# Padding the SBUF layout of a two-layer attention and feed-forward kernel to multiples of 64 bytes

## The chip, the cores and the metric

The program runs on one core of a Trainium2 chip. The metric is device time in microseconds (us), here the median of three runs. The profile is of one execution of the same program.

## The reference, cut to what matters

```python
x = x + _L0_xattn_ref(_layernorm(x), ctx_4096, Wq, bq, Wk, bk, Wv, bv, Wo, bo)  # 16-wide window, 8 heads
x = x + _L0_ffn_ref(_layernorm(x), Wg, Wu, Wd, ag, au, ad)                      # silu(gate) * up, inner width 1376
x = x + _L1_xattn_ref(_layernorm(x), ctx_4096, ctx_4096, pos, mask, Wq, Wk, Wv, Wo)  # 32 heads, 8 key/value heads, rotary
x = x + _L1_ffn_ref(_layernorm(x), gate_w, expert_w)                            # top 2 of 8 experts
```

`x` is 16 x 64 tokens of 512 float32 values, that is 8 tiles of 128 tokens. All four steps keep float32 accuracy.

## The kernel before, in words

The kernel is four stages in a row, each with its own order of work for every engine: `window_attention`, `gated_ffn`, `cross_attention` and `routed_ffn`. All large products are made by the helper `mm3` (lines 121 to 123): each operand is kept as a high and a low part of type float32r, and three matmuls (high by high, high by low, low by high) give the accurate product. A matmul names its stationary operand first (the weights that are loaded into the array) and its moving operand second (the one that streams through). The profile writes them the other way round: `PS<-NTh,W` has NTh moving and W stationary. Each matmul of the kernel has its own weight load.

The forms that the prediction speaks of, all with 128 x 128 stationary operands:

- **Keys and values** of the cross attention: `wkv` moves (256 columns), the context `CTh`/`CTl` is stationary.
- **Queries** of the cross attention: the normed rows `NTh`/`NTl` move (256 columns), the weights in `W` are stationary.
- **Output** of the cross attention: `W` moves (512 columns), `ca_aTh`/`ca_aTl` is stationary.
- **Gate and up** of the gated feed-forward: `NTh`/`NTl` move (512 columns), `W` is stationary. **Down**: `W` moves (512 columns), a part of `W` or `ff_hl` is stationary.
- **Experts** of the routed feed-forward: `W` moves (512 columns), `NTh`/`NTl` is stationary.

The cross attention is a loop over 64 units (8 key/value groups by 8 tiles), software-pipelined so that in one turn TensorE makes the keys, values and queries of unit n, the scores of n-2, the attention product of n-3 and the output of n-4. The gated stage loops over 11 chunks of the inner width, the routed one over 23 tiles of tokens. Between them the other engines split operands into parts (ACT high, DVE or POOL low), apply the rotary table and the softmax, and load weights (SP's queue).

SBUF buffers are placed one behind the other in the order in which the program asks for them (`two_layers_kernel`, from line 1994), each at the next multiple of 32 bytes within a partition; what a stage asks for is given back at its end. `X` begins at byte 16512, a multiple of 64. `const` has 164 floats (656 bytes) and begins at a multiple of 64 too, so what comes behind it begins 32 past one: `NTh` at 33568, then `NTl`, `CTh`, `CTl`. The six small buffers of `NormedRows.buffers` take 224 bytes, three and a half times 64, so `qT` (99328) and `room` (107520) are at multiples of 64 again. `room` has `GatedInputs.SIZE` = 3606 floats and turns the offset once more: `CTX` or `W` (121952), `ca_raw`, `ca_kvraw`, `ca_cosT`, `ca_sinT`, `ca_cap`, the `rf_gw` and `ca_wkv` parts, `ff_hl` and most buffers of the window attention begin 32 past a multiple of 64. In the cross attention `mx`, `su` and `rc` (96 bytes) bring `ca_aTh` and `ca_aTl` to a multiple of 64 (224832).

So before the change every float32r operand that moves through TensorE begins 32 bytes past a multiple of 64, and all of them step by multiples of 512 bytes within their buffer. Of the float32r stationary operands all do but `ca_aTh` and `ca_aTl`.

Of the kernel before, what the change touches and what calls it, by code (L numbers as in the profile page):

```python
# [20 lines left out]
F32 = mybir.dt.float32  # L21
F32R = mybir.dt.float32r
# [6 lines left out]
P = 128  # L29
BATCH, SEQ, E = 16, 64, 512  # L30
# [3 lines left out]


WARM_UP = 7
WH, WD, WIN = 8, 8, 16
BLK = 16
KEYS = 2 * BLK
# [5 lines left out]
IT = -(-INTER // P)  # L45

HEADS, KVH, HD = 32, 8, 128
GRP = HEADS // KVH
# [87 lines left out]
def views(room, *sizes):  # L136

    ends = np.cumsum(sizes).tolist()
    return [room[:, end - size:end] for end, size in zip(ends, sizes)]


def allocator(nc, stack):
    def sb(name, shape, dt=F32):
        return stack.enter_context(nc.sbuf_tensor(name, shape, dt))

    def sem(name):
        return stack.enter_context(nc.semaphore(name))

    return sb, sem
# [131 lines left out]
def window_attention(nc, sh, d, norm, ffn):  # L281
# [13 lines left out]
    with ExitStack() as st:  # L295
        sb, sem = allocator(nc, st)
# [44 lines left out]
        S = {x: sem("wa_" + x) for x in names}  # L341

        with nc.Block() as block:
            @block.sync
            def _(sp):
                def load(dst, name, done, a, b):
                    sp.dma_start(dst[:, a:b, :], d[name][2 * a:2 * b, :, :].rearrange("(t b) s e -> (b s) t e", b=2)
                                 ).then_inc(done[a], 16)

                load(sh.X, "x", x_loaded, *LOADS[0])  # L350
                sp.dma_start(sh.const[:], d["consts"][:, :C_BASE]).then_inc(S["const_loaded"], 16)
                for i, w in enumerate(("Wq", "Wk", "Wv", "Wo")):
                    sp.dma_start(wrow[:, i, :], d["L0_" + w]).then_inc(S["loaded"], 16)
                    sp.dma_start(brow[i:i + 1, :], d["L0_b" + w[1]].rearrange("(a c) -> a c", a=1)).then_inc(S["loaded"], 16)
                load(sh.CTX, "ctx", ctx_loaded, *LOADS[0])
                for b2 in range(2):
                    sp.dma_start(bv_row[:, b2 * SEQ:(b2 + 1) * SEQ], d["L0_bv"].rearrange("(a c) -> a c", a=1)
                                 ).then_inc(S["bv_loaded"], 16)
                load(sh.X, "x", x_loaded, *LOADS[1])
                load(sh.CTX, "ctx", ctx_loaded, *LOADS[1])  # L360
                sp.wait_ge(S["zeroed"], 2)
                sp.wait_ge(S["const_loaded"], 16)
                sp.dma_start(d["blank"][0:P, :], blank[:]).then_inc(S["const_loaded"], 16)
                sp.wait_ge(S["const_loaded"], 32)
                for k in range(1, 4):
                    sp.dma_start(d["blank"][k * P:(k + 1) * P, :], blank[:]).then_inc(S["const_loaded"], 16)
                ffn.first_loads(sp)
                sp.wait_ge(S["const_loaded"], 80)

            @block.tensor  # L370
            def _(pe):


                pe.wait_ge(S["zeroed"], 1)
                for _ in range(WARM_UP):
                    nc.tensor.matmul(PJ, wT[:, 0, :], wT[:].rearrange("p a b -> p (a b)"), start=True, stop=True)
# [375 lines left out]
class GatedInputs:  # L752

    SIZE = 7 * E + 2 * IT

    def __init__(self, nc, st, room, d):
        sem = allocator(nc, st)[1]
# [418 lines left out]
def cross_attention(nc, sh, d, norm, next_norm, cross):  # L1178
# [11 lines left out]
    with ExitStack() as st:  # L1190
        sb, sem = allocator(nc, st)
# [10 lines left out]
        kT = kT.rearrange("p (a k) -> p a k", a=2)  # L1202

        qT = sh.qT[:].rearrange("p (a h b x) -> p a h b x", a=2, h=2, b=4)
        mx, su, rc = (sb("ca_" + x, [P, 2, 4]) for x in ("mx", "su", "rc"))
        aT = [sb(f"ca_aT{part}", [P, GRP, P], F32R) for part in ("h", "l")]

        QT = sh.PS[:, 0, :]
        KT = sh.PS[:, 1, 0:PAIR]
# [8 lines left out]
        S = {x: sem("ca_" + x) for x in names}  # L1218
# [775 lines left out]
def two_layers_kernel(nc, d):  # L1994
    with ExitStack() as st:
        sh = Shared()
        sh.X = st.enter_context(nc.sbuf_tensor("X", [P, TT, E], F32))
        sh.const = st.enter_context(nc.sbuf_tensor("const", [P, C_BASE], F32))
        sh.PS = st.enter_context(nc.psum_tensor("PS", [P, 8, 512], F32))
        sh.NTh, sh.NTl, sh.CTh, sh.CTl = (  # L2000
            st.enter_context(nc.sbuf_tensor(x, [P, EC, TT * P], F32R)) for x in ("NTh", "NTl", "CTh", "CTl"))
        d["blank"] = nc.dram_tensor("blank", (4 * P, E), F32).ap()
        d["slots"], d["outs"] = (nc.dram_tensor(x, (rows, E), F32).ap()
                                 for x, rows in (("slots", EXPERTS * CAP), ("outs", SLOT_TILES * P)))
        sh.norm_buffers = NormedRows.buffers(allocator(nc, st)[0])
        sh.qT = st.enter_context(nc.sbuf_tensor("qT", [P, 4 * E], F32))
        norm1, norm2 = (NormedRows(nc, sh, st, name, views(sh.qT, E, E, E, E)[2:]) for name in ("n1", "n2"))
        sh.room = st.enter_context(nc.sbuf_tensor("room", [P, GatedInputs.SIZE], F32))
        ffn = GatedInputs(nc, st, sh.room, d)
        with nc.sbuf_tensor("CTX", [P, TT, E], F32) as sh.CTX:  # L2010
            spent = window_attention(nc, sh, d, norm1, ffn)
        sh.W = st.enter_context(nc.sbuf_tensor("W", [P, RING, 2, EC, E], F32R))
        cross = CrossInputs(nc, sh, st, d)
        q_rows = views(sh.qT, E, E, E, E)
        norm3 = NormedRows(nc, sh, st, "n3", q_rows[:2] + views(cross.cosT, E, E) + views(cross.sinT, E, E) + q_rows[2:])
        gated_ffn(nc, sh, d, norm1, ffn, norm2, cross, spent)
        cross_attention(nc, sh, d, norm2, norm3, cross)
        routed_ffn(nc, sh, d, norm3, cross)
# [28 lines left out]
```

## Time and profile before

| | |
|---|---|
| median of 3 runs | 1142.0 us (1138.05, 1142.0 and 1142.47) |
| span of the profiled execution, first to last instruction | 1134.8 us |
| what the three timed runs have beyond that span | 3.3 to 7.7 us |
| busy PE, PEld (weight loads), DVE, ACT, POOL | 1043.0, 866.0, 662.1, 385.0, 499.3 us |
| mean granted TensorE clock | 0.965 of full speed |

The page names the profiled execution by its span and does not say which of the timed runs stands beside it, so its own time is that span plus an unknown few microseconds. Busy shares are read against the span. A matmul's own duration in the profile has a modelled end and overlaps the next one; how fast matmuls follow each other is read from their starts in the timeline.

### The profile page before, as it was taken

The numbers are of one execution on the slowest core, as the hardware profiler recorded it, in microseconds if no ns is written. First come the engines' busy times: TensorE is split into PE (matmuls) and PEld (weight loads), VectorE is DVE, ScalarE is ACT, GpSimd is POOL, SyncE is SP. The second block draws the span as 40 slices with busy tenths as digits, with TensorE's granted clock in tenths as the row PEclk, the third lists the DMA queues.
The fourth block names the chain that finished last, engine by engine and source line by source line (L and its number), as shares of the span: only waits on it lengthen the run. The fifth ranks groups of instructions, "written<-read, shape, count | busy, mean of one in ns | idle before, by whom it ended". The sixth has DMA issues, their size and how long they took to land. (4 is left out here: it accounts for less than half of the span.)

```text
span 1134.8 us, 24062 instructions
## 1 busy us (share of the span) xinstructions
PE 1043.0 (92%) x9170; PEld 866.0 (76%) x9170; DVE 662.1 (58%) x1383; ACT 385.0 (34%) x875; POOL 499.3 (44%) x567
## 2 busy tenths in 40 slices
PE   7889888999999889999999999999999999755994
PEld 3666677788887678888888888888888888533783
DVE  5787874544454676556565655656565565850324
ACT  4687864222222332222222222222222221520331
POOL 3444441342223345545444554444454542137745
PEclk9899998999999889999999999999999999986997
DMA  6100004573642021111111011111011100036768
GB/s 227 33 3 4 3 4 122 186 262 134 234 149 85 10 84 29 51 34 45 31 29 48 29 28 57 28 49 28 29 47 28 38 11 1 1 115 208 248 219 275
DMA packets 51807, 92.07 MB, mean 81 GB/s; under 512 B 10749, under 2 KB 24317, under 8 KB 51261
## 3 DMA queue, kind: packets, MB, share of 16 engines
q1 hardware_dynamic: 42108, 69.13, 19.5%
q10 hardware_dynamic: 6624, 12.06, 3.2%
q0 software_dynamic: 2976, 9.44, 2.5%
q8 instruction: 76, 1.25, 0.5%
q14 instruction: 23, 0.18, 0.1%
HBM read 77.25 MB, written 36.18 MB: 100 GB/s over the span
## 5 line engine op out<-in xcount | busy, mean ns | idle before, releaser
L121 PE MATMUL PS<-NTh,W 128*128 128x256 f32 (+2 forms) x688 | 216.7, 315 | 0.0
L123 PE MATMUL PS<-NTh,W 128*128 128x256 f32 (+2 forms) x688 | 214.1, 311 | 0.0
L122 PE MATMUL PS<-NTl,W 128*128 128x256 f32 (+2 forms) x688 | 214.1, 311 | 0.0
L122 PEld LDWEIGHTS PS<-NTl,W 128*128 128x128 f32 (+1 forms) x688 | 131.1, 191 | 7.0
L123 PEld LDWEIGHTS PS<-NTh,W 128*128 128x128 f32 (+1 forms) x688 | 129.3, 188 | 8.5
L121 PEld LDWEIGHTS PS<-NTh,W 128*128 128x128 f32 (+1 forms) x688 | 129.6, 188 | 7.2
L1509 POOL TENSOR_TENSOR W<-ca_raw,W 128x512 fp32r<-128x512 f32 x64 | 82.5, 1290 | 114.5 <-ACT W L1359 114.5
L1447 DVE TENSOR_REDUCE ca_su<-room 128x4 f32<-128x256 f32 x64 | 26.9, 420 | 155.4 <-ACT room L1375 155.4
L1476 DVE TENSOR_TENSOR room<-PS,ca_sinT 64x512 f32<-64x512 f32 (+1 forms) x192 | 115.1, 600 | 2.6
L121 PE MATMUL PS<-W,ca_aTh 128*128 128x512 f32 x256 | 106.3, 415 | 3.5 <-DVE X L1464 3.5
L1375 ACT ACTIVATE room<-room 128x256 f32<-128x256 f32 x64 | 26.8, 419 | 222.6 <-POOL room L1556 222.6
L122 PE MATMUL PS<-W,ca_aTh 128*128 128x512 f32 x256 | 100.9, 394 | 0.0
L123 PE MATMUL PS<-W,ca_aTl 128*128 128x512 f32 x256 | 100.6, 393 | 0.0
L1546 POOL TENSOR_TENSOR qT<-room 128x512 f32<-128x512 f32 x64 | 81.8, 1278 | 26.6 <-DVE room L1476 26.3
L1476 DVE TENSOR_TENSOR room<-PS,ca_cosT 128x512 f32<-128x512 f32 (+1 forms) x96 | 57.8, 603 | 56.4 <-PE PS L1298 55.9
L1006 DVE TENSOR_TENSOR X<-X,PS 128x512 f32<-128x512 f32 x88 | 60.3, 687 | 48.9 <-PE PS L123 48.4
L1049 POOL TENSOR_TENSOR ff_hl<-ff_hf,W 128x512 fp32r<-128x512 f32 (+1 forms) x22 | 28.6, 1302 | 134.0 <-ACT W L943 134.0
L1399 ACT ACTIVATE room<-PS 128x256 f32<-128x256 f32 x64 | 24.6, 385 | 182.1 <-PE PS L1324 182.1
L121 PE MATMUL PS<-ca_wkvh,CTh 128*128 128x256 f32 x256 | 78.9, 308 | 1.9 <-issue 1.7
L1533 POOL TENSOR_TENSOR room<-room,ca_rc 128x256 f32<-128x256 f32 x64 | 39.2, 613 | 82.2 <-DVE ca_rc L1449 82.2
L123 PE MATMUL PS<-ca_wkvh,CTl 128*128 128x256 f32 x256 | 72.1, 282 | 0.0
L122 PE MATMUL PS<-ca_wkvl,CTh 128*128 128x256 f32 x256 | 71.9, 281 | 0.0
(258 smaller groups left out, 2366.8 us busy)
## 6 DMA issues: line engine op xcount, KB each, us to landing
ca_raw<-in_L_Wq SPq DMA_DIRECT2D x32, 256.0 KB, 2.8
ca_raw<-in_L_Wo SPq DMA_DIRECT2D x32, 256.0 KB, 2.6
rf_raw<-in_experts SPq DMA_DIRECT2D x28, 256.0 KB, 3.6
room<-slots ACTq DMA_DIRECT2D x23, 256.0 KB, 3.2
outs<-room ACTq DMA_DIRECT2D x23, 256.0 KB, 3.3
outs<-blank SPq DMA_DIRECT2D x11, 512.0 KB, 8.9
room<-in_L_Wg SPq DMA_DIRECT2D x10, 256.0 KB, 2.7
room<-in_L_Wu SPq DMA_DIRECT2D x10, 256.0 KB, 3.0
```

The costliest lines, as they stand in the source:

```text
L121: nc.tensor.matmul(out, l_hi, r_hi, start=first, stop=False)
L122: nc.tensor.matmul(out, l_hi, r_lo, start=False, stop=False)
L123: return nc.tensor.matmul(out, l_lo, r_hi, start=False, stop=last)
L1006: nc.vector.tensor_tensor(sh.X[:, t, :], sh.X[:, t, :], D[:, t % 4, :], ALU.add).then_inc(S["added"], 1)
L1049: nc.gpsimd.tensor_tensor(hl[:w, slot, tok], hf[:w, half, :], hh[:w, slot, tok].bitcast(F32), ALU.subtract).then_inc(S["h_split"], 1)
L1375: nc.scalar.activation(s, s, ACT.Exp).then_inc(S["exped"], 1)
L1399: nc.scalar.activation(pT, PP, ACT.Copy).then_inc(S["pp_copied"], 1)
L1447: nc.vector.reduce_sum(su[:, w, :], sm[:, w, :, :], AX_X).then_inc(S["summed"], 1)
L1476: return nc.vector.tensor_tensor(out[out_rows, some].rearrange("p (m k) -> p m k", m=count), x[rows, :].rearrange("p (m k) -> p m k", m=co ...
L1509: return nc.gpsimd.tensor_tensor(dst[1], src, dst[0].bitcast(F32), ALU.subtract)
L1533: nc.gpsimd.tensor_tensor(s, s, rc[:, w, :].unsqueeze(2).broadcast_to([P, 4, SEQ]), ALU.mult).then_inc(S["probs"], 1)
L1546: last = nc.gpsimd.tensor_tensor(qT[:, slot, j, :, :].rearrange("p b (m q) -> p m b q", m=2), *parts, ALU.add)
```

## The change

Four buffers change size or place. `const` grows from 164 to 176 floats, with the load writing the first 164 as before; 8 floats that nobody uses follow the small buffers of the norm; `room` grows from 3606 to 3616 floats; and `ca_aTh`, `ca_aTl` are asked for ahead of `mx`, `su` and `rc` instead of behind them. No instruction is added, removed or moved in any queue.

```diff
+LINE = 16
...
-                sp.dma_start(sh.const[:], d["consts"][:, :C_BASE]).then_inc(S["const_loaded"], 16)
+                sp.dma_start(sh.const[:, 0:C_BASE], d["consts"][:, :C_BASE]).then_inc(S["const_loaded"], 16)
...
-    SIZE = 7 * E + 2 * IT
+    SIZE = -(-(7 * E + 2 * IT) // LINE) * LINE
...
+        aT = [sb(f"ca_aT{part}", [P, GRP, P], F32R) for part in ("h", "l")]
         mx, su, rc = (sb("ca_" + x, [P, 2, 4]) for x in ("mx", "su", "rc"))
-        aT = [sb(f"ca_aT{part}", [P, GRP, P], F32R) for part in ("h", "l")]
...
-        sh.const = st.enter_context(nc.sbuf_tensor("const", [P, C_BASE], F32))
+        sh.const = st.enter_context(nc.sbuf_tensor("const", [P, -(-C_BASE // LINE) * LINE], F32))
...
         sh.norm_buffers = NormedRows.buffers(allocator(nc, st)[0])
+        st.enter_context(nc.sbuf_tensor("norm_rest", [P, LINE // 2], F32))
```

By the sizes, `NTh` to `CTl` and the small buffers of the norm move by 32 bytes, `qT` and `room` by 64, and everything behind `room` by 96 (`W` to 122048). `NTh`, `NTl`, `CTh`, `CTl`, `CTX`, `W`, `ca_raw`, `ca_kvraw`, the tables, the `ca_wkv` parts, `ff_hl` and `rf_raw` come to multiples of 64; `X`, `const`, `qT`, `room` and `ca_aTh`, `ca_aTl` (224832 as before) stay at one. In the window attention the small `wa_wrow`, `wa_brow`, `wa_wT` and `wa_bias` go the other way, from a multiple of 64 to 32 past one.

## Rows read from the trace of the kernel before

**Rows 1.** The page: its first line and the busy time of each engine.

```profile
span 1134.8 us, 24062 instructions
PE 1043.0 (92%) x9170; PEld 866.0 (76%) x9170; DVE 662.1 (58%) x1383; ACT 385.0 (34%) x875; POOL 499.3 (44%) x567
```

**Rows 2.** Busy us by stretch, then granted clock, DMA share and GB/s.

```profile
core 0: us, PE busy (x) PEld busy (x) DVE busy (x) ACT busy (x) POOL busy (x), PEclk, DMA share, GB/s
...
250.00:360.00 110.00, 110.00 (x511) 89.15 (x510) 53.01 (x79) 27.54 (x44) 26.71 (x26) 1.00 0.48 167
...
500.00:600.00 100.00, 100.00 (x705) 87.47 (x704) 58.86 (x125) 26.57 (x85) 50.56 (x59) 1.00 0.13 37
...
1050.00:1100.00 50.00, 47.97 (x239) 39.31 (x238) 15.95 (x36) 18.84 (x32) 34.58 (x36) 1.00 0.76 242
```

**Rows 3.** PE groups by form: line, engine, moving,stationary, shape, count, busy us, modelled mean ns.

```profile
L122 PE MATMUL PS<-NTl,W 128*128 128x256 f32 x512 | 143.8, 281 | 0.0
...
L122 PE MATMUL PS<-W,ca_aTh 128*128 128x512 f32 x256 | 100.9, 394 | 0.0
...
L122 PE MATMUL PS<-ca_wkvl,CTh 128*128 128x256 f32 x256 | 71.9, 281 | 0.0
...
L122 PE MATMUL PS<-NTl,W 128*128 128x512 f32 x160 | 64.0, 400 | 0.0
...
L122 PE MATMUL PS<-W,NTh 128*128 x92 | 36.7, 399 | 0.0
...
L122 PE MATMUL PS<-W 128*128 128x512 f32 x80 | 31.7, 396 | 0.0
```

**Rows 4.** Timeline of PE in one unit of the cross attention: start us, duration us.

```profile
562.81 0.28 PE L122 MATMUL PS<-ca_wkvl,CTh 128*128 128x256 f32 x1
...
564.06 0.28 PE L121 MATMUL PS<-NTh,W 128*128 128x256 f32 x1
...
566.89 0.27 PE L1298 MATMUL PS<-const,room 128*128 128x128 f32 x1
567.00 1.00 PE L1314 MATMUL PS<-room,qT 128*128 128x64 f32 x8
567.84 0.39 PE L1324 MATMUL PS<-const,room 128*128 128x128 f32 x2
...
568.29 0.39 PE L122 MATMUL PS<-W,ca_aTh 128*128 128x512 f32 x1
...
570.62 0.39 PE L123 MATMUL PS<-W,ca_aTl 128*128 128x512 f32 x1
```

**Rows 5.** Timeline of PE in the gated feed-forward.

```profile
300.17 0.39 PE L123 MATMUL PS<-NTh,W 128*128 128x512 f32 x1
...
302.50 0.40 PE L121 MATMUL PS<-W 128*128 128x512 f32 x1
...
303.91 0.39 PE L121 MATMUL PS<-NTh,W 128*128 128x512 f32 x1
```

**Rows 6.** Timeline of PE in the routed feed-forward.

```profile
1041.58 0.63 PE L122 MATMUL PS<-W,NTh 128*128 x1
...
1044.99 0.61 PE L121 MATMUL PS<-W,NTh 128*128 x1
...
1050.01 0.40 PE L123 MATMUL PS<-W,NTl 128*128 x1
...
1052.08 0.40 PE L123 MATMUL PS<-W,NTl 128*128 x1
```

**Rows 7.** Busy us by stretch within the routed feed-forward, columns as in rows 2.

```profile
1043.20:1045.20 2.00, 2.00 (x6) 1.53 (x5) 0.00 (x0) 0.00 (x0) 2.00 (x3) 0.50 0.80 195
1046.00:1052.00 6.00, 6.00 (x32) 5.02 (x31) 0.69 (x1) 3.46 (x6) 4.37 (x6) 1.00 0.71 217
```

**Rows 8.** POOL groups by form: count, busy us, mean ns.

```profile
L1509 POOL TENSOR_TENSOR W<-ca_raw,W 128x512 fp32r<-128x512 f32 x64 | 82.5, 1290 | 114.5 <-ACT W L1359 114.5
L1546 POOL TENSOR_TENSOR qT<-room 128x512 f32<-128x512 f32 x64 | 81.8, 1278 | 26.6 <-DVE room L1476 26.3
```

**Rows 9.** DMA issues: count, KB each, median us to landing.

```profile
ca_raw<-in_L_Wq SPq DMA_DIRECT2D x32, 256.0 KB, 2.8
...
room<-in_L_Wg SPq DMA_DIRECT2D x10, 256.0 KB, 2.7
```

**Rows 10.** PE groups of the window attention whose moving operand is wa_wT.

```profile
L445 PE MATMUL PS<-wa_wT,CTX 128*128 128x128 f32 x96 | 18.3, 301 | 2.0 <-DVE X L604 1.3
...
L445 PE MATMUL PS<-wa_wT,wa_edge 128*128 128x128 f32 x32 | 6.6, 290 | 2.4 <-issue 2.3
```

## The prediction
> **What bounds the kernel now.** I read the page first. TensorE is busy for 1043.0 of the 1134.8 us and, its own weight loads aside, nothing else for over 58% of them [rows 1]. A share over the whole span hides stages, so the busy time by stretch comes next [rows 2]: in the gated feed-forward TensorE has work for 110.00 of 110.00 us, in the cross attention for 100.00 of 100.00, and in the routed stage for 47.97 of 50.00, with the full clock granted in each. DVE stands at 53, 59 and 16 us there and POOL at 27, 51 and 35. In these stages time is set by how fast matmuls follow each other; nobody waits for data.
>
> Then the groups of TensorE by form [rows 3]. They give the counts, one of three lines of the helper each, so times three: 1536 query matmuls of 256 columns, 768 for keys and values of 256, 768 for the output of 512, 480 for gate and up of 512, 240 for down of 512 and 276 for the experts of 512: 4068 in all. (The narrow last chunk of the gated stage is left out.) Their durations have modelled ends, so the pace comes from starts in the timeline:
>
> - keys and values: 562.81 to 564.06 is 11 gaps in 1.25 us, 113.6 ns [rows 4];
> - queries: 564.06 to 566.89 is 24 gaps in 2.83 us, 117.9 ns [rows 4];
> - output: 568.29 to 570.62, 10 gaps, 233 ns [rows 4];
> - gate and up: 300.17 to 302.50, 10 gaps, 233 ns; down: 302.50 to 303.91, 6 gaps, 235 ns [rows 5];
> - experts: 1050.01 to 1052.08, 9 gaps, 230 ns [rows 6].
>
> What the reader is to see is that these are slower than the array. The expert matmuls also run once at half clock (0.50) [rows 7]: 1041.58 to 1044.99 is 8 gaps in 3.41 us, 426.2 ns for the same 512 columns [rows 6]. Half of that is 213.1 ns, and 106.6 for 256 columns. At the full clock the same matmuls, from the same buffers, need 230. So at the full clock each form loses 7 to 22 ns a matmul that it does not lose at half the clock. Something feeds the array a little too slowly; the change can only touch how the operands are read. Weight loads are not it: eight matmuls of only 64 columns, each with 128 weight columns to load, start 567.00 to 567.84, 105 ns each [rows 4], below every gap in question.
>
> **The change, part by part.** It adds no instruction, wait or DMA, and moves none past another; only addresses change. The sum therefore has one real term.
>
> *float32r matmuls.* Every moving operand of the 4068 goes from 32 bytes past a multiple of 64 to a multiple of 64. No row shows a float32r operand moving from a multiple of 64, so the price is bounded from both sides. Least: nothing, if the lost nanoseconds have another cause. Most: the whole excess over the array's pace, 1536 x 11.3 + 768 x 7.0 + 768 x 19.9 + 480 x 19.9 + 240 x 21.9 + 276 x 16.9 ns = 17.4 + 5.4 + 15.3 + 9.6 + 5.3 + 4.7 = 57.7 us. Between them I take a mechanism that the rows can price: if operands are fetched in pieces of 64 bytes (16 float32 columns), a run that begins in the middle of a piece touches one piece more. Sixteen columns are 213.1 / 32 = 6.7 ns. The nearest row is that of keys and values: 106.6 + 6.7 = 113.3 against 113.6 measured. The others lose more, so this is not their whole story, and I do not count on the rest. 4068 x 6.7 ns = 27.1 us. It lies wholly on the path, in the stages where TensorE is never idle [rows 2]. What comes next there is far: a unit of the cross attention would shorten by (24 + 12 + 12) x 6.7 = 0.3 us, and DVE, next in line, has 41% of its time free.
>
> The Trainium skill speaks against this term ("SBUF — State Buffer", "SBUF: two separate sides"): it puts SBUF's lines at 16 bytes. No row here shows a line's size. By that rule the old addresses already begin a line, the term is zero and the time stays at 1142.
>
> The skill's "TensorE: Matmul & The Clock Gate" ("Back-to-back issue gap") gives N / 2.4 + 2.5 ns, that is 109.2 and 215.8 ns; the rows above are 4 to 19 ns slower. As an estimate by that page, an excess that vanished would leave about 1095 us.
>
> *Stationary operands.* They move to multiples of 64 as well, except `ca_aTh` and `ca_aTl`, which were there. Output, with its stationary operand at a multiple of 64, has 233 ns; the experts, with theirs 32 past one, 230 [rows 4, 6]. The aligned one is no faster, so: nothing.
>
> *Other engines and DMA.* POOL's subtraction into `W`, all 32 past, takes 1290 ns, its sum into `qT`, all at multiples, 1278 [rows 8]. Twelve nanoseconds on an engine with half its time free are nothing; if POOL were the path, 64 of them would be 0.8 us. 256 KB land in 2.8 us in `ca_raw` (32 past) and in 2.7 in `room` (at a multiple) [rows 9]: nothing.
>
> *The padding, and `wa_wT`.* The load of `const` has the same 128 rows. `wa_wT`, small, goes the wrong way: it moves through 96 + 32 matmuls [rows 10]; at one piece each that is 0.9 us, at the least nothing. These are plain float32 and in a stage with other waits; I take nothing.
>
> **Sum.** The profiled span is 1134.8 us; the median run lies 7.2 above it. 1134.8 - 27.1 = 1107.7 for the span, and with the same 7.2, 1115 us.
>
> **Rivals.**
>
> *Nothing happens.* The excess is the price of reading four bytes per column at the full clock, wherever the buffer starts. For: queries and keys begin at the same place within 64 bytes and yet differ by 4.3 ns, so alignment is not all of it; 512 columns lose 17 to 22 ns, where one piece would be 6.7. Against: no loss at all at half clock means that a small stall is being hidden there, just what an extra fetch would look like. Time: 1142, within 0.5%.
>
> *All of the excess goes.* The extra piece also unsettles what follows, and 57.7 us vanish: 1084. For: pace varies among forms that only differ in address. Against: the same variation is there at one alignment. I count this with the forecast's side and give it a fifth of that chance.
>
> *Slower: the two reads of TensorE fall into step.* While one operand moves, the next weights are read. For the output `W` is now 32 past and `ca_aTh` is not; afterwards both start alike, and so does everything else. If equal starts make the two reads meet, each form falls to the slowest pace that its width shows, 117.9 and 235 ns: 768 x 4.3 + 768 x 2 + 480 x 2 + 276 x 5 ns = 7.2 us, 1149 us. It decides once it costs over 5.7 us (0.5%). Against: the experts' two operands start alike already and are the fastest of the 512s [rows 6].
>
> *The change is not what it says.* If sizes were rounded otherwise, a buffer would still be 32 past. The sizes leave no doubt for `NTh` to `CTl` and `W`; I fold this into the first rival.
>
> **How the numbers follow.** Half a per cent, 5.7 us, is about what a measurement of this kernel can tell from no change. Forecast and its extreme (faster): 0.47, most of it the one-piece mechanism, with its own range 1085 to 1132. Nothing: 0.38. Slower: 0.15. Faster is the likeliest single case, so 1115. The range must reach into the first rival, so it ends at 1147, and at 1090 below, which leaves out the farthest part of the full excess (about 0.04) and the slower case (nearly 0.15).
>
> **What would show it.** Right: the gaps of queries near 111 ns, keys and values near 107, the 512s near 226, the same in all stages; the instruction count unchanged; the cross attention's 100 us of TensorE work still 100 of 100, with more units in it. Half-clock gaps stay at 426. If the gaps stay where they are, the read is not made in pieces of 64 bytes and the prediction is wrong; if gaps fall but the span does not, some wait has taken over, and it would show as idle time ahead of TensorE in the cross attention.

## The result and the profile after

The changed kernel takes 1145.96 us (median of 22 runs, 1139.38 to 1151.34) against 1141.38 us of the kernel before (22 runs beside them, 1138.05 to 1143.86). The ratio is 1.0043 with a 95% interval of 1.0031 to 1.0054: 4.9 us slower (3.5 to 6.2), within the half per cent that was set as the bound, and 31 us above the forecast.

The page of the changed kernel, span and first line of busy times (it answers to [rows 1]):

```profile
span 1144.8 us, 24062 instructions
...
PE 1056.0 (92%) x9170; PEld 877.2 (77%) x9170; DVE 661.0 (58%) x1383; ACT 386.0 (34%) x875; POOL 499.9 (44%) x567
```

The instruction count is the same to the last one. DVE, ACT and POOL differ by about 1 us. TensorE is busy for 13 us more with the same 9170 matmuls: the loss, whatever it is, lies in how long TensorE takes for them. (Not all 13 us belong to the change, see below.)

Busy time by stretch: the first 50 us, then the loop of the cross attention from the first to the last matmul of keys and values, then its last turns up to the last output matmul. First the kernel before, whose rows of these stretches were not shown yet (columns as in [rows 2]):

```profile
0.00:50.00 50.00, 39.03 (x561) 23.28 (x562) 31.66 (x68) 27.54 (x45) 20.31 (x36) 0.86 0.48 146
...
394.10:961.50 567.40, 559.68 (x3923) 490.26 (x3924) 346.50 (x741) 151.23 (x473) 274.19 (x308) 0.99 0.13 36
961.50:997.00 35.50, 27.66 (x159) 21.05 (x158) 26.22 (x68) 16.13 (x34) 5.66 (x9) 1.00 0.00 0
```

And the changed kernel:

```profile
0.00:50.00 50.00, 39.57 (x518) 22.54 (x518) 29.08 (x64) 25.74 (x41) 18.95 (x35) 0.83 0.47 146
...
395.90:969.00 573.10, 565.24 (x3923) 496.12 (x3924) 346.43 (x741) 152.26 (x473) 274.31 (x308) 0.99 0.12 36
969.00:1006.60 37.60, 31.82 (x160) 24.71 (x158) 26.20 (x68) 16.13 (x34) 5.60 (x9) 0.86 0.00 0
```

Read the middle rows first: 3923 matmuls in both, granted clock 0.99 in both, DVE, ACT and POOL alike to about 1 us, and yet 573.10 us instead of 567.40. TensorE's busy time grows by the same 5.6 us. No wait has appeared; the matmuls follow each other more slowly. The outer two rows are another matter: the granted clock is 0.83 against 0.86 at the start and 0.86 against 1.00 in the last turns. The two spans differ by 10 us, the medians by under 5: the profiled execution of the changed kernel had less of the full clock than that of the kernel before. (Every run of the two kernels on record lies 2.1 to 2.2 us above its own span, so these two took about 1137 and 1147 us, one well below its kernel's median, one a little above.) More of that further on.

The groups of TensorE by form, changed kernel (every line of the helper is one further down, so L123 here is L122 in [rows 3]):

```profile
L123 PE MATMUL PS<-NTl,W 128*128 128x256 f32 x512 | 143.8, 281 | 0.0
L123 PE MATMUL PS<-W,ca_aTh 128*128 128x512 f32 x256 | 102.5, 400 | 0.0
L123 PE MATMUL PS<-ca_wkvl,CTh 128*128 128x256 f32 x256 | 73.3, 286 | 0.0
L123 PE MATMUL PS<-NTl,W 128*128 128x512 f32 x160 | 63.6, 398 | 0.0
L123 PE MATMUL PS<-W,NTh 128*128 x92 | 37.3, 405 | 0.0
```

One form stands out: keys and values, 71.9 us before and 73.3 after, mean 281 and 286 ns, at the same number of matmuls. The queries are unchanged to the digit, gate and up are 2 ns better. The means of output and experts grow by 6 ns, but the output's contain a stretch at half clock in the last turns, and durations have modelled ends, so the starts decide. One turn of the cross attention in the changed kernel (start us, duration us; answers to [rows 4]):

```profile
562.76 0.40 PE L123 MATMUL PS<-W,ca_aTh 128*128 128x512 f32 x1
...
565.09 0.40 PE L124 MATMUL PS<-W,ca_aTl 128*128 128x512 f32 x1
...
566.27 0.28 PE L123 MATMUL PS<-ca_wkvl,CTh 128*128 128x256 f32 x1
...
567.58 0.28 PE L122 MATMUL PS<-NTh,W 128*128 128x256 f32 x1
...
570.30 0.28 PE L124 MATMUL PS<-NTh,W 128*128 128x256 f32 x1
...
575.34 0.28 PE L123 MATMUL PS<-ca_wkvl,CTh 128*128 128x256 f32 x1
```

Keys and values: 566.27 to 567.58 is 11 gaps in 1.31 us, 119.1 ns, where [rows 4] gave 113.6. Queries: 23 gaps in 2.72 us, 118.3 (before 117.9). Output: 10 gaps in 2.33 us, 233, as before. The whole turn, from one unit's second key matmul to the next one's, takes 9.07 us; in the kernel before it is 562.81 [rows 4] to 571.79, 8.98 us:

```profile
571.79 0.28 PE L122 MATMUL PS<-ca_wkvl,CTh 128*128 128x256 f32 x1
```

From here on the gap of a form is the mean distance of successive starts within its runs over the whole trace (620 gaps of keys and values, some 1470 of queries, 620 to 640 of output, 450 of gate and up, 222 of down, 220 of experts):

| ns | keys, values | queries | output | gate, up | down | experts |
|---|---|---|---|---|---|---|
| before | 114.4 | 117.6 | 232.6 | 233.2 | 234.3 | 229.8 |
| after | 119.3 | 118.5 | 232.2 | 231.9 | 234.4 | 231.8 |
| times count | 768 x 4.9 | 1536 x 0.9 | 768 x -0.4 | 480 x -1.3 | 240 x 0.1 | 276 x 2.0 |
| us | +3.8 | +1.4 | -0.3 | -0.6 | 0.0 | +0.6 |

The sum is +4.8 us, and the ratio gives +4.9. So these six numbers account for the result, and the first for some four fifths of it. What remained was why keys and values slowed down when both their operands came to multiples of 64.

### The profile page after: what moved, and what is told of

It is laid out like the page before. It is cut to its first block and busy times, and to the rows that moved or that the text cites. A ratio compares the mean times of both kernels' runs of the same rounds, so it can differ in the third digit from the quotient of the medians.

```text
span 1144.8 us, 24062 instructions
## 1 busy us (share of the span) xinstructions
PE 1056.0 (92%) x9170; PEld 877.2 (77%) x9170; DVE 661.0 (58%) x1383; ACT 386.0 (34%) x875; POOL 499.9 (44%) x567
## 3 DMA queue, kind: packets, MB, share of 16 engines
q8 instruction: 76, 1.25, 0.4%
## 5 line engine op out<-in xcount | busy, mean ns | idle before, releaser
L122 PE MATMUL PS<-NTh,W 128*128 128x256 f32 (+2 forms) x688 | 217.6, 316 | 0.0
L123 PE MATMUL PS<-NTl,W 128*128 128x256 f32 (+2 forms) x688 | 213.7, 311 | 0.0
L122 PEld LDWEIGHTS PS<-NTh,W 128*128 128x128 f32 (+1 forms) x688 | 130.3, 189 | 6.9
L123 PEld LDWEIGHTS PS<-NTl,W 128*128 128x128 f32 (+1 forms) x688 | 130.2, 189 | 6.9
L122 PE MATMUL PS<-W,ca_aTh 128*128 128x512 f32 x256 | 107.9, 422 | 3.3 <-DVE X L1465 3.3
L123 PE MATMUL PS<-W,ca_aTh 128*128 128x512 f32 x256 | 102.5, 400 | 0.0
L122 PE MATMUL PS<-ca_wkvh,CTh 128*128 128x256 f32 x256 | 79.9, 312 | 2.5 <-issue 2.4
L123 PE MATMUL PS<-ca_wkvl,CTh 128*128 128x256 f32 x256 | 73.3, 286 | 0.0
```

What stands on the lines that cost most here:

```text
L122: nc.tensor.matmul(out, l_hi, r_hi, start=first, stop=False)
L123: nc.tensor.matmul(out, l_hi, r_lo, start=False, stop=False)
```

## The experiments

Two theories stood at the start. The first: what counts is the **alignment** of each operand to 64 bytes, only with the other sign than forecast. The second: what counts is the **distance** between the two operands of a matmul. The change moves buffers by different amounts (NTh to CTl by 32 bytes, everything behind room by 96), so it changes the distance from CTh to wkv and from NTh to W by 64; moving everything by the same 32 bytes would align it and leave the distances.

### One padding alone: everything aligned, distances kept

```diff
+LINE = 16
...
-                sp.dma_start(sh.const[:], d["consts"][:, :C_BASE]).then_inc(S["const_loaded"], 16)
+                sp.dma_start(sh.const[:, 0:C_BASE], d["consts"][:, :C_BASE]).then_inc(S["const_loaded"], 16)
...
-        sh.const = st.enter_context(nc.sbuf_tensor("const", [P, C_BASE], F32))
+        sh.const = st.enter_context(nc.sbuf_tensor("const", [P, -(-C_BASE // LINE) * LINE], F32))
```

> Only const is padded, so everything behind it moves by 32 bytes alike: NTh to CTl and W, the wkv parts and so on begin at multiples of 64, and the distances between them are those of before. Theory A, the distance between the operand that moves and the weights that are read meanwhile sets the pace: nothing changes, keys and values stay at 113.6 ns a matmul, the time at 1141 us. Theory B, beginning at a multiple of 64 is itself what costs: keys and values at 119 to 120 ns as after the change, about 1146 us. My forecast's theory (64-byte pieces) is out by the result; it would say 107 ns and 1115 us.

1139.99 us (12 runs) against 1139.81 (21 runs), ratio 1.0008 (0.9991 to 1.0025). The turn in this kernel's timeline:

```profile
562.80 0.28 PE L123 MATMUL PS<-ca_wkvl,CTh 128*128 128x256 f32 x1
...
564.06 0.28 PE L122 MATMUL PS<-NTh,W 128*128 128x256 f32 x1
...
571.80 0.28 PE L123 MATMUL PS<-ca_wkvl,CTh 128*128 128x256 f32 x1
```

Eleven gaps in 1.26 us, a turn of 9.00 us; all six mean gaps are within 0.4 ns of the kernel before. Here every moving operand has come from 32 past a multiple of 64 to a multiple of 64, just as the prediction wanted, and so has every stationary one but aT, which goes the other way. Nothing happens. The alignment theory is out, and so is the forecast's mechanism.

### The distances alone, without alignment

```diff
         sh.room = st.enter_context(nc.sbuf_tensor("room", [P, GatedInputs.SIZE], F32))
+        st.enter_context(nc.sbuf_tensor("behind_room", [P, 16], F32))
```

> The kernel before with 64 bytes behind room: W, wkv and all that follows move by 64, NTh to CTl stay. Nothing becomes a multiple of 64 that was none, but the distance between CTh and wkv, and between NTh and W, changes by 64 as in the change. Theory A: keys and values at 119 to 120 ns, queries about 0.5 ns slower, 1145 to 1146 us. Theory B: all gaps as before, 113.6 and 117.9 ns, 1141 us.

1146.49 us (6 runs) against the same 1139.81, ratio 1.0061 (1.0037 to 1.0085). No float32r operand in front of or behind the padding changes its place within 64 bytes. In this kernel's timeline:

```profile
563.74 0.28 PE L122 MATMUL PS<-ca_wkvl,CTh 128*128 128x256 f32 x1
...
565.06 0.28 PE L121 MATMUL PS<-NTh,W 128*128 128x256 f32 x1
```

Eleven gaps in 1.32 us: 120 ns, the slow pace of the changed kernel, with everything still 32 past a multiple of 64. The same with half as much padding:

```diff
+        st.enter_context(nc.sbuf_tensor("behind_room", [P, 8], F32))
```

> The kernel before with 32 bytes behind room: W, wkv and so on come to multiples of 64, NTh to CTl stay 32 past one, the distances change by 32. Theory A: a third pace for keys and values, anywhere from 109 to 120 ns, and 1137 to 1147 us. Theory B: what moves decides, so keys and values (wkv moves) at 119 to 120 ns, queries (NTh moves) as before, about 1146 us.

1144.45 us (10 runs), ratio 1.0045 (1.0028 to 1.0062); keys and values 118.5 ns, queries 118.4, experts 233.4, down 230.3. Each distance gives paces of its own, for each form another.

Down does not fit this. Its moving operands and the stationary ones of two of its three matmuls lie in W together, and ff_hl, the third, a fixed way behind, so no layout changes these distances. Yet its gap is 234.3 ns before, 232.0 with 64 bytes behind room and 230.3 with 32. In the kernel with const alone padded W and ff_hl begin, by the sizes, at the very addresses of this last one, and there it is 234.3. What differs between those two is where const ends and where NTh to CTl, qT and room begin. So the distance of a matmul's own two operands is not all that sets its pace; what else does was not tested.

### The distance by itself: a map

A kernel with nothing but matmuls: twelve equal ones in a row for each pair of starts, `S` stationary, `M` moving, 256 or 512 columns, and for comparison weights of 8 columns. No part of the reference is computed.

```python
for n, w, ss, ms in ((256, 128, range(0, 128, 8), range(0, 128, 8)),
                     (512, 128, range(0, 128, 16), range(0, 128, 16)),
                     (256, 8, (0,), range(0, 128, 8)),
                     (512, 8, (0,), range(0, 128, 8))):
    for s in ss:
        mark(160 + s // 4)
        for m in ms:
            mark(32 + m // 4)
            last = run(s, m, w, n)
```

> No part of the reference: twelve equal float32r matmuls at a time, for every pair of start offsets within 512 bytes in steps of 32 (256 columns) or 64 (512 columns), and the same with only 8 weight columns. Theory A: the pace depends on the difference of the two offsets, from about 109 to 120 ns for 256 columns, and with 8 weight columns on nothing. Theory B: pairs with the moving operand at a multiple of 64 are slower by 6 ns whatever the weights' offset, also with 8 weight columns. If neither matters in this plain setting, all pairs have one pace.

674.03 us for the whole map. In its timeline a row of 12 is one block; the single matmul ahead of it tells by its width where the block's operands begin (width less 160 for the weights, at the head of a row of the map, and width less 32 for the moving operand, times 16 bytes):

```profile
166.33 0.29 PE L45 MATMUL PS<-M,S 128*128 128x172 f32 x2
...
172.59 0.18 PE L45 MATMUL PS<-M,S 128*128 128x40 f32 x1
172.62 1.63 PE L50 MATMUL PS<-M,S 128*128 128x256 f32 x12
...
175.62 0.18 PE L45 MATMUL PS<-M,S 128*128 128x44 f32 x1
175.64 1.67 PE L50 MATMUL PS<-M,S 128*128 128x256 f32 x12
```

Both blocks have weights that begin 192 bytes past a multiple of 256; the moving operand begins at 128 in the first and at 192 in the second. All starts are multiples of 64, and the blocks take 1.63 and 1.67 us. By starts that is 114.7 and 118.8 ns a matmul. The whole map shows three things. It repeats every 256 bytes in either start, up to four pairs that differ by some 4 ns. Matmuls of 256 columns take 113.3 to 120.3 ns, and the fast ones (up to 115 ns) are mostly those whose moving operand begins 64 bytes ahead of the weights, modulo 256: 26 of the 32 such pairs, and five others. Matmuls of 512 columns take 226.7 to 233.9, and the fastest are mostly those with equal starts. With weights of only 8 columns the 256-column matmuls take 113.3 at starts of 64, 128, 160, 192 and 224 and some 116.7 at 0, 32 and 96; the 512-column ones nearly always 231 to 232.6. So less weight reading does not bring the array's pace of 106.6 and 213.1 ns back, and a start at a multiple of 64 does not decide there either. The expectation that with 8 columns nothing hangs on the starts missed. But the number of weight columns counts too: with the weights at 0 and the moving operand at 128, 128 weight columns give 118.9 ns and 8 give 113.3.

Equal matmuls in a row are not what the kernel does. The second map repeats the five address sequences of the kernel (the four 128-row blocks, high and low parts) for eight starts and eight distances each. Again nothing of the reference is computed.

```python
def keys(a, b):
    for c in range(4):
        for (s, m) in ((0, 0), (0, 1), (1, 0)):
            yield a + c * 1024 + s * 4096, 128, b + c * 256 + m * 2048, 256
```

> No part of the reference: the five sequences of addresses that the kernel uses (keys and values, queries, output, gate and up, experts) without any other engine at work, for eight starts of either operand within 256 bytes. Theory A: each sequence's pace depends on the distance; keys and values show 113.5 at 64 before and 119 to 120 at equal starts, as in the two kernels. Queries at the distance of before (moving 64 ahead of the weights): 117.8 as in the kernel if the addresses alone make the pace, 114 as in the plain map if something else in the kernel slows them.

884.91 us. Two blocks of keys and values whose context begins 32 bytes past a multiple of 256 (widths as above: 34 means wkv at 32, 46 means wkv at 224):

```profile
42.41 0.18 PE L46 MATMUL PS<-M,S 128*128 128x34 f32 x1
42.43 1.68 PE L93 MATMUL PS<-M,S 128*128 128x256 f32 x12
...
51.62 0.19 PE L46 MATMUL PS<-M,S 128*128 128x46 f32 x1
51.66 1.63 PE L93 MATMUL PS<-M,S 128*128 128x256 f32 x12
```

Distance 0: 1.68 us. Distance 192, which is the kernel before: 1.63. The full answer, mean gaps in ns over the eight starts, by distance modulo 256 (by the starts that the sizes give, no trace shows an address: wkv less CTh for keys, W less NTh for queries, gate and experts, W less aT for output; one number where the starts agree within about 1.5 ns either way):

| form | 0 | 32 | 64 | 96 | 128 | 160 | 192 | 224 |
|---|---|---|---|---|---|---|---|---|
| keys, values | 119 | 117.5 | 118 | 119.5 | 119 | 118.5 | **114.5** | 118 |
| queries | 119.8 | 118.3 | **113.6 to 117.8** | 118 | 118.5 | 119.8 | 117.8 | 117 |
| output | **226.6 to 232.1** | 233 | **229.5** | 233.7 | 232.4 | 234 | 233.2 | 232.8 |
| gate, up | **226.6 to 231.3** | 232.8 | 233.1 | 234 | 232 | 233.6 | **229.6** | 233.3 |
| experts | **226.7 to 232.1** | 233 | **229.5** | 233.6 | 232.4 | 234 | 233.2 | 232.8 |

(Of keys at a start of 0, the first two blocks are left out, which ran at 1.2 GHz with up to 213 ns a matmul, and the third, the only one of eight at distance 64 with 113.3.) Now set the kernels into it. Before: distances 192 for keys, 64 for queries, gate and experts, 32 for output; the table says 114.5, up to 117.8, 233.1, 229.5, 233, and the kernel has 114.4, 117.6, 233.2, 229.8, 232.6. After: 0, 128 and 128; the table says 119, 118.5, 232, 232.4 and 232.4 for the output, and the kernel has 119.3, 118.5, 231.9, 231.8, 232.2. Matmuls alone, with no other engine at work, reproduce both kernels to within about 1 ns, with one exception: at the start that NTh has in the kernel before (32), the block of the queries took 113.9 ns, and the kernel has 117.6. By the expectation above something in the kernel beside these addresses slows that form; what it is stays open. Down is not in the map.

### Keys and values put back, and put wrong

The changed kernel with wkv alone moved to where its distance is 192 again:

```diff
+        sb("ahead_wkv", [P, 48])
         wkv = [sb(f"ca_wkv{part}", [P, 2, EC, KVC], F32R) for part in ("h", "l")]
+        sb("behind_wkv", [P, 16])
```

> The changed kernel with 192 bytes ahead of the wkv parts and 64 behind them: wkv again begins 64 bytes before CTh modulo 256, as before the change, all starts stay multiples of 64, and the distance of ca_aTh to W is that of the changed kernel modulo 256. Theory A (distance modulo 256 sets the pace): keys and values back from 119.5 to 113.6 ns, 768 x 5.9 = 4.5 us less than the changed kernel, 1141 us, no difference from before. Rival, the loss lies elsewhere (in the window attention's small buffers, in waits): keys and values may return, the time stays at 1146.

Keys and values are back at 114.1 ns, the other five forms stay as in the changed kernel. The loop of the cross attention, in busy time by stretch of this kernel, with the last turns behind it:

```profile
396.00:964.60 568.60, 560.25 (x3923) 491.30 (x3924) 346.50 (x741) 151.32 (x473) 274.20 (x308) 1.00 0.13 36
964.60:1005.00 40.40, 33.12 (x159) 25.59 (x158) 26.32 (x68) 16.06 (x34) 5.66 (x9) 0.83 0.00 0
```

573.10 us have become 568.60, that is 4.5 of the 5.7 us that the loop had lost; by the gaps, 768 x 5.2 ns, it is 4.0, and the granted clock here is 1.00 against 0.99. The time is 1143.1 us (12 runs) against 1140.75 (29 runs), ratio 1.0023 (1.0008 to 1.0039), +2.6 us where 1141 was expected: about half of the loss came back in the timed runs, not four fifths. The sum by gaps leaves +0.9 us (queries +1.4, experts +0.6, output and gate -0.9), at the lower edge of the interval of 0.9 to 4.4.

So the opposite was run as well: the kernel **before** with nothing but wkv moved to distance 0.

```diff
+        sb("ahead_wkv", [P, 16])
         wkv = [sb(f"ca_wkv{part}", [P, 2, EC, KVC], F32R) for part in ("h", "l")]
+        sb("behind_wkv", [P, 48])
```

> The kernel before with one thing of the change alone: the wkv parts move by 64 bytes (16 floats ahead of them, 48 behind, so that all buffers further on move by 256 bytes in all), so that the context (stationary) and wkv (moving) begin at equal places modulo 256 bytes as in the changed kernel. No buffer comes to a multiple of 64 that wasn't there. Theory 'distance modulo 256': gaps of keys and values go from 114.4 to 119.3 ns, all other forms stay; 768 x 4.9 ns = +3.8 us, ratio about 1.003. Rival 'the loss belongs to the alignment to 64 or to something else that moves with room': ratio 1.000, gaps as before.

1145.44 us (12 runs) against 1141.27 (23 runs), ratio 1.0034 (1.0021 to 1.0047): +3.9 us, 3.8 expected. In its timeline:

```profile
566.55 0.28 PE L122 MATMUL PS<-ca_wkvl,CTh 128*128 128x256 f32 x1
...
567.86 0.28 PE L121 MATMUL PS<-NTh,W 128*128 128x256 f32 x1
...
575.61 0.28 PE L122 MATMUL PS<-ca_wkvl,CTh 128*128 128x256 f32 x1
```

Eleven gaps in 1.31 us, a turn of 9.06 us: the changed kernel's rows (1.31 and 9.07), from a kernel in which no buffer has come to a multiple of 64. Queries, gate, down and experts keep the paces of before to 0.1 ns, the output is 0.5 slower. These 64 bytes between the context and wkv are four fifths of the result.

### Better distances

The table promises more than the kernel before uses: the output at distance 0 instead of 32.

```diff
-        mx, su, rc = (sb("ca_" + x, [P, 2, 4]) for x in ("mx", "su", "rc"))
+        sb("ahead_aT", [P, 32])
         aT = [sb(f"ca_aT{part}", [P, GRP, P], F32R) for part in ("h", "l")]
+        mx, su, rc = (sb("ca_" + x, [P, 2, 4]) for x in ("mx", "su", "rc"))
```

> The kernel before with ca_aTh and ca_aTl alone moved by 32 bytes, so that they begin where W does modulo 256 (32 apart before). By the map of the small kernel, 512 columns go at 227 ns at equal starts and at 231 to 233 otherwise. Theory A: output from 232.5 to 227 ns, 768 x 5.5 = 4.2 us less, 1136 us. Rival, in the kernel this form is held up by other engines' traffic: output stays at 232, the time at 1140.

The output's gap falls from 232.6 to 229.1 ns as the map says, keys and values rise by 0.6. The sum is -2.2 us. Measured: 1141.12 us (12 runs) against 1140.75, ratio 1.0 (0.998 to 1.0021), that is 0.0 us with -2.3 to +2.4. The expectation of 1136 missed. The gap is gained, the time is not shown to be; the interval only just allows the sum.

Then all of them at once: NTh, W and aT alike modulo 256, wkv 64 bytes ahead of the context, everything 32 past a multiple of 64. By the map queries lose a little (distance 0 instead of 64), output and gate gain, and experts hardly change.

```diff
         sh.room = st.enter_context(nc.sbuf_tensor("room", [P, GatedInputs.SIZE], F32))
+        st.enter_context(nc.sbuf_tensor("behind_room", [P, 48], F32))
...
+        sb("ahead_wkv", [P, 16])
...
-        mx, su, rc = (sb("ca_" + x, [P, 2, 4]) for x in ("mx", "su", "rc"))
+        sb("ahead_aT", [P, 16])
         aT = [sb(f"ca_aT{part}", [P, GRP, P], F32R) for part in ("h", "l")]
+        mx, su, rc = (sb("ca_" + x, [P, 2, 4]) for x in ("mx", "su", "rc"))
```

> The kernel before with paddings that make NTh, W and ca_aTh begin alike modulo 256 and wkv 64 before CTh; all of them are 32 past a multiple of 64 as before. Theory A by the map: gate and up from 233.5 to 227 ns (3.4 us), output to 227 (4.2 us), experts from 230 to 227 (0.8 us), keys and values as before, queries from 117.8 to 119.5 (2.6 us more): in sum 5.8 us less, 1134 us. Theory B (multiples of 64 decide, either way): no change, 1140 us. If queries do not follow the map in the kernel, the sum is up to 2.6 us better.

1137.01 us (12 runs) against 1140.75 (29 runs), ratio 0.9973 (0.996 to 0.9986). It beats both kernels: by the ratio 3.1 us below the one before. One turn of it:

```profile
560.26 0.28 PE L122 MATMUL PS<-ca_wkvl,CTh 128*128 128x256 f32 x1
...
561.51 0.28 PE L121 MATMUL PS<-NTh,W 128*128 128x256 f32 x1
...
565.78 0.39 PE L122 MATMUL PS<-W,ca_aTh 128*128 128x512 f32 x1
...
568.07 0.39 PE L123 MATMUL PS<-W,ca_aTl 128*128 128x512 f32 x1
```

Keys and values 11 gaps in 1.25 us (113.6 ns), output 10 in 2.29 (229). Mean gaps: 113.7, queries 119.3, output 229.1, gate and up 229.8, down 230.2, experts 229.1. The sum is -0.5 + 2.6 - 2.7 - 1.6 - 1.0 - 0.2 = -3.4 us. Expected were -5.8, with output and gate at 227; and the 1.0 of down was not expected at all.

Last, the same distances with everything at multiples of 64, built from the changed kernel:

```diff
         sh.room = st.enter_context(nc.sbuf_tensor("room", [P, GatedInputs.SIZE], F32))
+        st.enter_context(nc.sbuf_tensor("behind_room", [P, 32], F32))
...
+        sb("ahead_wkv", [P, 16])
         wkv = [sb(f"ca_wkv{part}", [P, 2, EC, KVC], F32R) for part in ("h", "l")]
+        sb("behind_wkv", [P, 16])
```

> The changed kernel, everything at a multiple of 64 as there, with padding (32 floats behind room, 16 ahead of wkv, 16 behind it) that gives it the distances of e6_all_distances: NTh, W and aT begin alike modulo 256, wkv 64 bytes before the context. Theory 'distance modulo 256 alone': the gaps and the time of e6_all_distances: K 114, Q 119, O 229, gate and up 230, down 230, experts 229 ns; about -3.7 us against the kernel before, ratio 0.997, in spite of the other alignment. Rival 'the alignment costs something too' (the part of the loss that e4_after_wkv_back did not return): 1.000 or above.

The gaps are those of the kernel just before within 0.7 ns (113.8, 119.3, 229.8, 229.9, 230.1, 229.7), 0.8 to 5.5 ns away from those of the changed kernel. The map is off here: at these starts, 64, its blocks took 226.6, 227.7 and 226.7 ns for output, gate and experts. The time is 1139.83 us (12 runs) against 1141.27 (23 runs), ratio 0.9987 (0.9971 to 1.0002): better than the changed kernel, whose interval begins at 1.0031, but -1.5 us instead of the expected -3.7; the sum of its own gaps is -2.6, inside its interval of -3.3 to +0.2.

### The sums together

| kernel | distances mod 256: keys; W less NTh; W less aT | sum of gaps, us | measured, us (95%) |
|---|---|---|---|
| after | 0; 128; 128 | +4.8 | +4.9 (3.5 to 6.2) |
| const alone | 192; 64; 32 | 0.0 | +0.9 (-1.0 to 2.8) |
| 64 bytes behind room | 0; 128; 32 | +5.1 | +7.0 (4.2 to 9.7) |
| 32 bytes behind room | 224; 96; 32 | +4.9 | +5.1 (3.2 to 7.1) |
| after, wkv put back | 192; 128; 128 | +0.9 | +2.6 (0.9 to 4.4) |
| before, aT like W | 192; 64; 0 | -2.2 | 0.0 (-2.3 to 2.4) |
| all distances | 192; 0; 0 | -3.4 | -3.1 (-4.6 to -1.6) |
| before, keys' distance 0 | 0; 64; 32 | +4.2 | +3.9 (2.4 to 5.4) |
| all distances, aligned | 192; 0; 0 | -2.6 | -1.5 (-3.3 to 0.2) |

The sum is (gap less gap before) times count over the six forms; measured is (ratio less 1) times the median of before. Nine sums, nine intervals that hold them, three of them at or near an edge. Where sum and measured time differ by more than half a microsecond, the measured one is the longer, by 0.9 to 2.2 us. One cause of that size is visible. In the profiled executions the last turns of the cross attention have a granted clock of 1.00 in some kernels, 0.86 to 0.91 in others, and 0.83 in two (64 bytes behind room, and wkv put back, shown above). What the engine did ahead of such a fall is to be seen in the changed kernel's timeline:

```profile
975.99 0.70 PE L1349 MATMUL PS<-room 64*128 64x256 f32 x4
979.17 1.34 PE L235 MATMUL PS<-const,qT 128*128 128x128 f32 x8 [2.48 <-DVE qT L224]
...
983.33 0.63 PE L124 MATMUL PS<-W,ca_aTl 128*128 128x512 f32 x1
983.76 0.63 PE L122 MATMUL PS<-W,ca_aTh 128*128 128x512 f32 x1
```

And in the kernel before, in the same place:

```profile
971.66 1.22 PE L234 MATMUL PS<-const,qT 128*128 128x128 f32 x8 [2.49 <-DVE qT L223]
```

In the changed kernel TensorE idles for 2.48 us for DVE, and the output matmuls behind it start 430 ns apart: the lower of the two levels, 1.2 GHz, where 2.4 GHz gave 233. The kernel before idles for 2.49 us and keeps the full clock in its profiled execution. So the same idle time can end either way. Over the runs of the kernel before that stood beside the experiments the mean granted clock lies anywhere between 0.959 and 0.969, and the time between 1135.6 and 1144.2 us; of the 10 us between the two spans at the top an estimated 4 are of this kind (10.0 less the loop's 5.7). Whether a layout makes the fall likelier stays open.

## Why the prediction was wrong

**What bounds the kernel** was right, and it is what made everything else readable. The changed loop has the same 3923 matmuls at the same clock, no new idle time, and gap times count gives the time within every interval, for better (all distances) as for worse.

**The step that failed is the one real term**: one 64-byte piece more per matmul, 4068 x 6.7 = 27.1 us. With const padded alone, every one of these operands begins at a multiple of 64 and the gaps change by 0.4 ns at most: the term is nothing, its lower bound. The argument for it was that keys and values, 113.6 ns, lie almost exactly one piece above the array's 106.6. The size was no accident, but its reading was wrong: the best pairs of the map take 113.3 and 226.7 ns, that is 6.7 and 13.6 above 106.6 and 213.1, about one sixteenth of the matmul at either width. An extra piece at the start would cost the same at 256 and 512 columns. The loss of the 512s, 17 to 22 ns, was named in the prediction as what speaks for "nothing happens", and should have been weighed there: a loss that grows with the length does not come from a start out of line. What the runs showed in its place is a pace that hangs on where the two operands of a matmul lie to each other modulo 256 bytes: keys and values at 119.3 ns instead of 114.4, 3.8 of the 4.9 us.

The rule of the Trainium skill that spoke against the term ("SBUF — State Buffer", "SBUF: two separate sides", lines of 16 bytes, so nothing is gained) comes out right here: 1.0008 for alignment alone. No run shows the line's size.

That 1145.96 us lies inside the range of 1090 to 1147 is luck: the range went that far up to take in a rival in which nothing changes, and the slower case, the way the time went, was to lie outside it.

**Weight loads are not it** went too far. Eight matmuls of 64 columns, 105 ns apart and of plain float32, show that a load fits into every gap, not that its reading leaves the moving operand alone. In the first map the number and the place of the weights change the pace: 118.9 against 113.3 ns for 128 and 8 columns, 114.7 against 120.0 for weights at 192 and at 128 with the moving operand at 128.

**Stationary operands: nothing** was wrong in its reasoning. Output and experts were compared by their place within 64 bytes, the aligned one being no faster. What differed was something else: W less aT was 32 modulo 256 and W less NTh 64, and the map puts 233 and 229.5 ns on these. Sorting by one quantity with the other free told nothing.

**The slower rival** had the right kind of mechanism: both reads of TensorE belong together, and equal starts make keys and values slow. It gave 7.2 us, of which 4.3 x 768 = 3.3 for keys and values; measured are 4.9 and 3.8. It was given 0.15 because the experts, whose operands "start alike already", were the fastest. They started alike modulo 64 only. Modulo 256 they were 64 bytes apart, one of the fast distances, and context and wkv were 192 apart, the only fast one of theirs. The rival also had equal starts as bad for all forms; for the 512s they are mostly the best. Its general form, "any distance may be better or worse, and the change moves distances by 64", was open to anyone who subtracted the addresses, and would have been worth more than 0.15.

**Nothing happens**, at 0.38, was nearest by its bound of half a per cent, but the loss is clear of zero (3.5 to 6.2 us), and its reason, the same price wherever a buffer begins, is wrong. Its argument that queries and keys differ at one alignment was the clue that alignment is not what counts.

**Other engines, DMA, padding, wa_wT at nothing** held: DVE, ACT and POOL are within 1.1 us over the span, and with const alone, which moves all of them too, the ratio is 1.0008.

The signs that were named ahead did their work: gaps of queries near 111 and keys near 107 never came, "if the gaps stay where they are, the read is not made in pieces of 64 bytes". No sign had been named for a gap that grows.

## What to carry to other kernels

When TensorE is the bound, look at the pace within each form of matmul (from starts, not durations) and at the distance of its two operands modulo 256 bytes; on this kernel that distance is worth up to 5 ns a matmul for float32r (up to 7 in the maps), alignment to 64 nothing. Measure each form again afterwards: down changed its pace with no change of its own distances. Padding for alignment also moves buffers against each other, so subtract the addresses of every pair that works together before and after, and keep the distances that are fast. Here two paddings ahead of wkv and aT and one behind the shared room gave 0.9973 (0.996 to 0.9986) of the time before, with all these starts 32 past a multiple of 64.

## What was not expected of the hardware

- The pace of float32r matmuls depends on the distance of the two operands modulo 256 bytes: 113.3 to 120.3 ns for 256 columns, 226.6 to 234.6 for 512 in the maps, where all other engines rest. 256 columns are mostly fastest with the moving operand 64 bytes ahead of the weights, 512 mostly with equal starts.
- The Trainium skill ("TensorE: Matmul & The Clock Gate", "Step-by-step: what each phase is for") has two independent read ports in TensorE, so that loading the next weights takes nothing from the running matmul. The maps speak against that for float32r: with the moving operand at 128, weights at 192 give 114.7 ns and weights at 128 give 120.0. But weights of 8 columns, which have little to read, also leave 113.3 to 116.9 and some 231, so it is not weight reading alone. The mechanism stays open.
- No distance reached the array's pace: the best are 113.3 and 226.6 ns, a sixteenth above 106.6 and 213.1.
- Some pairs have two paces. Queries at distance 64 take 113.6 to 114.1 ns at four of eight starts in the map and 117.6 to 117.8 at the others. The kernel before, at a start whose block in the map took 113.9, has 117.6. Why it does not find the faster one, worth up to 1536 x 3.7 = 5.7 us, was not settled.
- Down, whose operands keep their distances in every layout, takes 234.3 ns with const alone padded and 230.3 with 32 bytes behind room, at the same addresses of its own. What sets its pace stays open.
